# Cross-attention: keys scaled ahead of the last mask, the second chunk's transposes and evictions ahead of the values product, and a loop body of four batches

## The chip, the cores and the metric

The kernel runs on one core of a Trainium2 chip. A core has TensorE (PE, matrix products into the PSUM banks), VectorE (DVE), ScalarE (ACT), GpSimd (POOL) and SyncE (SP, which issues the transfers). Each engine works through a list of instructions of its own, in order, and semaphores tie the lists together. The metric is the device time of one launch in microseconds (us). The reader of a trace must know one habit of it: on PE an instruction's recorded duration overlaps the next one's start (a 512-column product is recorded as 0.39 us, and the next starts 0.23 us after it), so what PE loses is read from starts, or as recorded idle time plus that overlap of 0.17 us.

## What is computed

A decoder layer on 16 batches of 100 tokens, width 512: self-attention, cross-attention over 361 context tokens, and a routed feed-forward, each with a residual and a layer norm. The change touches cross-attention only:

```
q = rmsnorm((x @ Wq + bq) as 16 heads of 128) * qn_w
k = rmsnorm((ctx @ Wk + bk) as 4 heads of 128) * kn_w      # each shared by 4 query heads
v = (ctx @ Wv + bv) as 4 heads of 128
probs = softmax(q @ k^T / sqrt(128) + mask)
x = layernorm(x + (probs @ v) @ Wo)
```

## The kernel before

The program has three stages, one after another: self-attention, which also makes and stores the queries of cross-attention; cross-attention; feed-forward. In cross-attention the weights stay in SBUF and a loop runs over the 16 batches. Every product of precision is made in three passes, since each operand is kept as a high and a low part (`product3`, line 68): high x high, high x low, low x high. That is why each eviction comes twice: ACT writes the high part (`kTh`, `oTh`, `pTh`, `Vh`), then DVE subtracts it from the bank and writes the low part (`kTl`, `oTl`, `pTl`, `Vl`).

`body(j, par)` is written out by hand for each engine. It handles batch j in four steps s = 0 to 3, one for each of the four key heads and its four query heads. In a step, PE makes the scores of the four heads, and between them transposes the probabilities of the step before, in three chunks of 121 context tokens. DVE evicts each head's scores with the mask and takes the row's extreme (`masked`, line 1113), ACT takes the exponential and its sum (`exponent`, line 1010), DVE inverts the sums of two heads at a time (`invert_sums`, line 1119), and POOL scales the probabilities. After the fourth scores, PE makes the values product of the step before (`values_product`, three chunks by three passes, 9 matmuls), which ACT (line 1051) and DVE (line 1176) evict, and output products with `Wo` fill PE's time between.

The keys and values of the next batch are made inside the same steps, in three chunks c = 0, 1, 2 of 121 tokens. A key chunk goes this way:

- `keys(j + 1, c)` on PE, into one of two banks. Chunks 1 and 2 use the same bank, so chunk 2 waits until DVE has read chunk 1 (semaphore `k_ev`).
- `key_squares` on DVE: adds the bias (line 1076, which frees the bank), sums the squares (line 1081).
- `key_rsqrt` on POOL.
- `key_norm` on DVE (line 1089): scales the 121x512 chunk, 0.67 us.
- `transpose_keys` on PE (line 887): four transposes.
- `keys_hi` on ACT (line 995) and `keys_lo` on DVE (line 1095). The next batch's first scores wait for all three `keys_lo` (semaphore `kt_lo`).

In step 2 the chunk-0 keys are scaled, transposed, and then `keys(j + 1, 2)` is made. In step 3 chunks 1 and 2 are scaled and transposed. DVE also finishes the layer norm of the batch before: `apply_norm` (line 1240) in step 3, whose result SP stores (`x2_d`, line 818), and at the end of step 3 DVE waits until that store has landed (semaphore `x2_out`, line 1186), because it will write the same buffer again.

`over_batches` (line 727) sets which bodies are written out: batches 0 and 1, then a loop `Fori` of six rounds with two batches each (2 to 13), then 14, 15 and the rest of the last one. Every engine runs this loop with a branch of its own at line 732, taken five times and passed through the sixth time. Between the two branches of one round PE's list has 1,171 instructions (a matmul counted with its weight load), DVE's 312, ACT's 153, POOL's 123 and SP's 47. The loop of the self-attention stage (line 175) holds 218 on DVE.

## Time and profile before

| | us |
|---|---|
| median of 3 runs | 1598.19 |
| the runs | 1594.86 to 1598.56 |
| the profiled execution, its own time | 1600.98 |
| its span, first to last instruction | 1599.2 |
| self-attention, about | 0 to 530 |
| cross-attention, about | 530 to 1377 |
| feed-forward, about | 1377 to 1599 |

Over the span PE is busy 1475.6 us, its weight loads 1206.4, DVE 954.0, ACT 663.1 and POOL 649.0. The views used are the groups of waits of one engine, the timeline (instructions in order of time, with the idle time before one and what ended it in brackets), busy time by stretch, and the DMA queues of a stretch. Branches, register operations and waits that stand alone have no row in the timeline. They are seen only as idle time before the next row.

In the loop a batch takes 51 to 52 us, and batches 4, 6, 8, 10 and 12 are those that come right after a taken branch.

### The profile page before, as it was taken

How to read it: one execution, taken by the hardware profiler on the slowest of the kernel's cores; microseconds unless marked ns; L12 is line 12 of the kernel's file. 1: busy time of each engine (PE TensorE's matmuls, PEld its weight loads, DVE VectorE, ACT ScalarE, POOL GpSimd, SP SyncE). 2: the span in 40 equal slices, each digit the busy share in tenths (PEclk: the TensorE clock that was granted, in tenths of full speed). 3: DMA queues.
4: the chain of work that ended last, by engine and by line, in shares of the span. 5: the costliest groups of instructions: out<-in, count | busy, mean ns of one | idle time of the engine just before them, and what ended most of it. 6: DMA issues, size and time to landing. Idle time of an engine off the chain costs nothing. (4 is left out here: it accounts for less than half of the span.)

```text
span 1599.2 us, 27710 instructions
## 1 busy us (share of the span) xinstructions
PE 1475.6 (92%) x8462; PEld 1206.4 (75%) x8462; DVE 954.0 (60%) x3585; ACT 663.1 (41%) x1789; POOL 649.0 (41%) x1000
## 2 busy tenths in 40 slices
PE   6999999999988679999999999999999999479967
PEld 6777877877866468888888887888888888367844
DVE  3666566566566475566655665556555665753457
ACT  4443343333342253444444443444444445333346
POOL 1334334334334164344434444344434443364164
PEclk8999999999999899999999999999999999679988
DMA  6221221221232332111121212111121212465463
GB/s 207 105 73 62 92 72 61 92 72 61 88 111 73 123 111 71 57 59 55 42 60 55 64 39 64 60 55 54 42 60 55 64 48 105 174 195 152 143 215 103
DMA packets 60957, 139.75 MB, mean 87 GB/s; under 512 B 10182, under 2 KB 21034, under 8 KB 59876
## 3 DMA queue, kind: packets, MB, share of 16 engines
q1 hardware_dynamic: 56296, 123.85, 23.3%
q0 software_dynamic: 4576, 14.95, 3.5%
q8 instruction: 31, 0.51, 0.1%
q14 instruction: 54, 0.44, 0.1%
HBM read 94.31 MB, written 44.46 MB: 87 GB/s over the span
## 5 line engine op out<-in xcount | busy, mean ns | idle before, releaser
L1248 POOL TENSOR_TENSOR b_pcarry<-b_half 128x1 f32<-128x1 f32 x173 | 47.9, 277 | 394.5 <-DVE b_rinv L1119 356.9
L1010 ACT ACTIVATE b_probs<-b_probs,b_nmax 100x361 f32<-100x361 f32 x256 | 152.0, 594 | 81.3 <-DVE b_nmax L1113 80.9
L68 PE MATMUL bank<-b_kTh,b_q 128*100 128x362 f32 x512 | 171.6, 336 | 10.7 <-DVE b_kTl L1095 5.9
L1113 DVE CUSTOM_DVE_ANT_0 b_probs<-bank,b_mask 100x361 f32<-100x361 f32 x256 | 135.3, 529 | 53.8 <-issue 45.1
L1273 POOL TENSOR_SCALAR b_probs<-b_probs,b_rinv 100x361 f32<-100x361 f32 x256 | 163.1, 650 | 0.0
L1106 DVE TENSOR_TENSOR b_pTl<-bank,b_pTh 121x400 fp32r<-121x400 f32 x192 | 109.8, 572 | 49.1 <-ACT b_pTh L1005 49.0
L1005 ACT ACTIVATE b_pTh<-bank 121x400 fp32r<-121x400 f32 x192 | 96.8, 504 | 87.7 <-PE bank L849 82.9
L1051 ACT ACTIVATE b_oTh<-bank,b_bv 128x400 fp32r<-128x400 f32 x64 | 38.0, 594 | 228.8 <-PE bank L68 228.8
L849 PE MATMUL bank<-b_ident,b_probs 100*121 100x100 f32 x768 | 110.3, 266 | 6.6 <-POOL b_probs L1273 6.6
L849 PEld LDWEIGHTS bank<-b_ident,b_probs 100*121 100x121 f32 x768 | 108.0, 186 | 8.8 <-POOL b_probs L1273 7.9
L68 PE MATMUL bank<-b_Woh,b_oTh 128*100 128x512 f32 x256 | 111.4, 435 | 1.9 <-DVE b_oTl L1176 1.9
L68 PEld LDWEIGHTS bank<-b_kTh,b_q 128*100 128x100 f32 x512 | 84.8, 166 | 30.5 <-issue 13.6
L68 PE MATMUL bank<-a_Wqh,a_x1Th 128*100 128x512 f32 x256 | 100.8, 394 | 2.6 <-DVE a_qn L539 1.4
L68 PE MATMUL bank<-b_Woh,b_oTl 128*100 128x512 f32 x256 | 101.1, 395 | 0.0
L68 PE MATMUL bank<-b_Wol,b_oTh 128*100 128x512 f32 x256 | 101.0, 395 | 0.0
L68 PE MATMUL bank<-a_Wqh,a_x1Tl 128*100 128x512 f32 x256 | 101.0, 395 | 0.0
L68 PE MATMUL bank<-a_Wql,a_x1Th 128*100 128x512 f32 x256 | 100.6, 393 | 0.0
L1176 DVE SCALAR_TENSOR_TENSOR b_oTl<-bank,b_bv,b_oTh 128x400 fp32r<-128x400 f32 x64 | 40.5, 633 | 100.3 <-ACT b_oTh L1051 100.3
L416 ACT ACTIVATE a_probs<-a_probs,a_nmax 100x100 f32<-100x100 f32 x256 | 92.8, 366 | 4.4 <-DVE a_nmax L492 4.4
L619 POOL TENSOR_TENSOR a_probs<-a_probs,a_rinv 100x400 f32<-100x400 f32 x64 | 54.7, 855 | 93.0 <-DVE a_rinv L499 93.0
L68 PE MATMUL bank<-b_Wkh,b_ctxh 128*121 128x512 f32 x192 | 81.7, 426 | 11.3 <-DVE b_kn L1076 8.2
L68 PE MATMUL bank<-b_kTl,b_q 128*100 128x362 f32 x256 | 83.9, 328 | 0.0
(255 smaller groups left out, 3958.3 us busy)
## 6 DMA issues: line engine op xcount, KB each, us to landing
q_d<-a_qo SPq DMA_DIRECT2D x64, 400.0 KB, 2.4
b_q<-q_d SPq DMA_DIRECT2D x64, 400.0 KB, 3.1
b_ctxr<-in_ctxT SPq DMA_DIRECT2D x48, 242.0 KB, 3.8
y_d<-c_y SPq DMA_DIRECT2D x32, 256.0 KB, 3.6
c_Eraw<-in_expert_w SPq DMA_DIRECT2D x10, 512.0 KB, 12.2
a_stage<-in_Wq SPq DMA_DIRECT2D x4, 1024.0 KB, 6.0
stage<-in_Wo SPq DMA_DIRECT2D x8, 512.0 KB, 4.6
a_xTr<-in_xT SPq DMA_DIRECT2D x8, 400.0 KB, 3.2
```

Source lines behind the costliest of these rows:

```text
L68: mm = eng.matmul(out, lhsT=l(c), rhs=r(c), start=first and k == 0, stop=last and k == n - 1)
L416: e = act.activation(probs[:, r, c, :], probs[:, r, c, :], ACT.Exp, scale=-1.0, bias=nmax[:, h:h + 1], accum_out=psums[:, r, c:c + 1])
L619: pool.tensor_tensor(probs[:, r], probs[:, r], rinv[:, r].unsqueeze(2).to_broadcast([S, DC, S]), ALU.mult).then_inc(pn_rdy, 1)
L849: mm = pe.transpose(t_bank[c % 2][0:KT, h * S:(h + 1) * S], probs[:, s % 2, h, c * KT:(c + 1) * KT], ident_s[0:S, 0:S])
L1005: act.activation(pTh[:, c, :], t_bank[c % 2][0:KT, 0:XG * S], ACT.Copy).then_inc(pt_hi, 1)
L1010: act.activation(p, p, ACT.Exp, scale=-1.0, bias=nmax[:, s % 2, h:h + 1], accum_out=psums[:, s % 2, h:h + 1]).then_inc(e_rdy, 1)
L1051: act.activation(oTh[:, kv, :], o_bank[:, 0:XG * S], ACT.Identity, bias=bv_s[:, kv:kv + 1]).then_inc(o_hi, 1)
L1106: dve.tensor_tensor(pTl[:, c, :], t_bank[c % 2][0:KT, 0:XG * S], pTh[:, c, :].bitcast(F32), ALU.subtract).then_inc(pt_lo, 1)
L1113: dve.tensor_tensor_reduce(out=probs[:, s % 2, h, 0:SE], in0=s_bank[h % 2][0:S, 0:SE], in1=mask_s[:], scale=-1.0, scalar=BIG, op0=ALU.add, ...
L1176: dve.scalar_tensor_tensor(out=oTl[:, kv, :], in0=o_bank[:, 0:XG * S], scalar=bv_s[:, kv:kv + 1], in1=oTh[:, kv, :].bitcast(F32), op0=ALU.add,
L1248: pool.tensor_tensor(pcarry[:, k:k + 1], half_s[:, 0:1], half_s[:, 0:1], ALU.add)
L1273: pool.tensor_scalar(p, p, rinv[:, s % 2, h:h + 1], 1.0, ALU.mult, ALU.mult).then_inc(p_rdy, 1)
```

## The change

Three edits, all in cross-attention.

1. DVE, steps 2 and 3: `key_norm` of the next batch's chunk 0 (step 2) or chunk 1 (step 3) moves from behind the fourth `masked` and the first `invert_sums` to in front of that `masked`.
2. Step 3: the transposes of key chunk 1 move in front of the values product on PE, its `keys_hi` in front of the values product's eviction on ACT, its `keys_lo` in front of that on DVE. Chunk 2 stays where it was.
3. The loop takes four batches a round and three rounds, so its branch is taken twice. Its rounds then hold 2,337 instructions on PE, 618 on DVE, 299 on ACT, 241 on POOL and 91 on SP.

```diff
-            with eng.Fori(0, B // 2 - 2) as pair:
-                body(2 * pair + 2, 0)
-                body(2 * pair + 3, 1)
+            with eng.Fori(0, (B - 4) // 4) as quad:
+                for k in range(4):
+                    body(4 * quad + 2 + k, k % 2)
...
                     if s == 3:
                         output(j, 1, range(1, 2))
+                        if not last:
+                            transpose_keys(j + 1, 1)
                     if before:
                         values_product(n - 1, (s + 3) % 4, j)
...
                     if s == 3:
                         if not last:
-                            transpose_keys(j + 1, 1)
                             transpose_keys(j + 1, 2)
                         output(j, 1, range(2, XG))
...
+                    if s == 3 and not last:
+                        keys_hi(j + 1, 1, 1 - par)
                     if before:
                         kv = (s + 3) % 4
                         act.wait_ge(o_done, n)
...
                     if s in (2, 3) and not last:
-                        keys_hi(j + 1, s - 2, 1 - par)
-                    if s == 3 and not last:
-                        keys_hi(j + 1, 2, 1 - par)
+                        keys_hi(j + 1, 2 * (s - 2), 1 - par)
...
                     if now:
+                        if s in (2, 3) and not last:
+                            key_norm(j + 1, s - 2)
                         masked(j, s, 3)
                         invert_sums(j, s, 0)
-                        if s in (2, 3) and not last:
-                            key_norm(j + 1, s - 2)
                         invert_sums(j, s, 2)
...
                     if s == 3 and not last:
                         key_norm(j + 1, 2)
+                        keys_lo(j + 1, 1, 1 - par)
                     if before:
...
                     if s == 3 and not last:
-                        keys_lo(j + 1, 1, 1 - par)
                         keys_lo(j + 1, 2, 1 - par)
```

What this does to the lists is shown at three places. Line numbers of the changed kernel run one or two higher.

DVE in step 2, before, from the last `pTl` of the step to the bias add of key chunk 1 (the ISA rows of line 1113 are `masked`):

```order
L1106 TENSOR_TENSOR b_pTl<-bank,b_pTh 121x400 [waits b_pt_hi]
L1111 REGISTER_ALU
L1112 MEMSET b_carry 100x1 [waits b_s_done]
L1113 ISA b_probs,b_nmax<-bank,b_mask 100x361
L1113 ISA b_nmax 100x1
L1119 RECIPROCAL b_rinv<-b_psums 100x2 [waits b_e_rdy]
L1087 REGISTER_ALU
L1089 TENSOR_TENSOR b_kn<-b_kn,b_krs 121x512 [waits k_rs]
L1119 RECIPROCAL b_rinv<-b_psums 100x2 [waits b_e_rdy]
L1075 REGISTER_ALU
L1076 TENSOR_TENSOR b_kn<-bank,b_bk 121x512 [waits k_done]
```

and in the changed kernel:

```order
L1107 TENSOR_TENSOR b_pTl<-bank,b_pTh 121x400 [waits b_pt_hi]
L1088 REGISTER_ALU
L1090 TENSOR_TENSOR b_kn<-b_kn,b_krs 121x512 [waits k_rs]
L1112 REGISTER_ALU
L1113 MEMSET b_carry 100x1 [waits b_s_done]
L1114 ISA b_probs,b_nmax<-bank,b_mask 100x361
L1114 ISA b_nmax 100x1
L1120 RECIPROCAL b_rinv<-b_psums 100x2 [waits b_e_rdy] x2
L1076 REGISTER_ALU
L1077 TENSOR_TENSOR b_kn<-bank,b_bk 121x512 [waits k_done]
```

The scaling of the keys now stands ahead of the fourth `masked`, and the two reciprocals stand side by side.

DVE at the end of step 3, before, down to the loop's branch:

```order
L1240 TENSOR_SCALAR b_y<-b_y,b_mv,b_rstd 100x512 [waits b_rstd_set]
L1087 REGISTER_ALU
L1089 TENSOR_TENSOR b_kn<-b_kn,b_krs 121x512 [waits k_rs]
L1175 REGISTER_ALU
L1176 SCALAR_TENSOR_TENSOR b_oTl<-bank,b_bv,b_oTh 128x400 [waits b_o_hi]
L1095 TENSOR_TENSOR b_kTl<-bank,b_kTh 128x4x121 [waits kt_hi] x2
L732 REGISTER_ALU [waits x2_out]
L732 COMPARE_AND_BRANCH
```

and in the changed kernel:

```order
L1241 TENSOR_SCALAR b_y<-b_y,b_mv,b_rstd 100x512 [waits b_rstd_set]
L1088 REGISTER_ALU
L1090 TENSOR_TENSOR b_kn<-b_kn,b_krs 121x512 [waits k_rs]
L1096 TENSOR_TENSOR b_kTl<-bank,b_kTh 128x4x121 [waits kt_hi]
L1177 REGISTER_ALU
L1178 SCALAR_TENSOR_TENSOR b_oTl<-bank,b_bv,b_oTh 128x400 [waits b_o_hi]
L1096 TENSOR_TENSOR b_kTl<-bank,b_kTh 128x4x121 [waits kt_hi]
L732 REGISTER_ALU [waits x2_out]
L732 COMPARE_AND_BRANCH
```

One of the two `kTl` now stands ahead of `oTl`. The branch still stands behind a wait for the store.

PE in step 3, before, from the end of the values product on:

```order
L68 MATMUL bank<-b_pTh,b_Vl 128x400
L887 MATMUL bank<-b_ident,b_kn 128x121 [waits kt_lo,k_rdy]
L887 MATMUL bank<-b_ident,b_kn 128x121 x3
L887 MATMUL bank<-b_ident,b_kn 128x121 [waits k_rdy]
L887 MATMUL bank<-b_ident,b_kn 128x121 x3
L68 MATMUL bank<-b_Woh,b_oTh 100x512
```

and in the changed kernel, ahead of it:

```order
L68 MATMUL bank<-b_Woh,b_oTl 100x512
L887 MATMUL bank<-b_ident,b_kn 128x121 [waits kt_lo,k_rdy]
L887 MATMUL bank<-b_ident,b_kn 128x121 x3
L856 REGISTER_ALU
L68 MATMUL bank<-b_pTh,b_Vh 128x400 [waits b_o_lo,b_pt_lo]
L68 MATMUL bank<-b_pTl,b_Vh 128x400
```

Four of the eight transposes now come before the nine matmuls of the values product, the other four stay behind them. PE's six output matmuls still end the step.

## Rows read from the trace of the kernel before

**Rows 1.** The page: engines' busy time over the span, share and instructions.

```profile
PE 1475.6 (92%) x8462; PEld 1206.4 (75%) x8462; DVE 954.0 (60%) x3585; ACT 663.1 (41%) x1789; POOL 649.0 (41%) x1000
```

**Rows 2.** Busy by stretch: PE, PEld, DVE, ACT, POOL; then PE's clock, DMA.

```profile
850.00:950.00 100.00, 98.23 (x541) 82.77 (x540) 59.55 (x222) 41.61 (x107) 43.64 (x82) 1.00 0.19 56
```

**Rows 3.** PE's waits, 560 to 1370 us: total, times, longest.

```profile
PE bank L68 <- DVE b_kn L1076: 8.2, 15, 3.5
...
PE bank L68 <- DVE b_kTl L1095: 4.2, 12, 0.4
PE bank L68 <- DVE b_nmax L1113: 3.8, 5, 1.1
...
PE bank L887 <- DVE b_kn L1089: 1.9, 1, 1.9
```

**Rows 4.** Timeline, PE, batch 5, step 2: start, duration, instruction, idle before.

```profile
841.04 0.39 PE L68 MATMUL bank<-b_Woh,b_oTl 128*100 128x512 f32 x1
841.36 0.63 PE L887 MATMUL bank<-b_ident,b_kn 121*128 121x121 f32 x4
842.33 0.47 PE L68 MATMUL bank<-b_Wkh,b_ctxh 128*121 128x512 f32 x1 [0.34 <-DVE b_kn L1076]
```

**Rows 5.** Timeline, DVE and one row of ACT, the same step.

```profile
839.42 0.57 DVE L1106 TENSOR_TENSOR b_pTl<-bank,b_pTh 121x400 fp32r<-121x400 f32 x1 [0.40 <-ACT b_pTh L1005]
840.10 0.53 DVE L1113 CUSTOM_DVE_ANT_0 b_probs<-bank,b_mask 100x361 f32<-100x361 f32 x1
...
840.63 0.68 DVE L1089 TENSOR_TENSOR b_kn<-b_kn,b_krs 121x512 f32<-121x512 f32 x1
841.39 0.17 DVE L1119 RECIPROCAL b_rinv<-b_psums 100x2 f32<-100x2 f32 x1
841.49 0.69 DVE L1076 TENSOR_TENSOR b_kn<-bank,b_bk 121x512 f32<-121x512 f32 x1
...
841.17 0.18 ACT L1010 ACTIVATION_READ_ACCUMULATOR b_probs<-b_probs,b_nmax 100x1 f32 x1
```

**Rows 6.** Timeline, batch 5, end of step 3: DVE, ACT, PE.

```profile
854.31 0.67 DVE L1089 TENSOR_TENSOR b_kn<-b_kn,b_krs 121x512 f32<-121x512 f32 x1
855.93 0.64 DVE L1176 SCALAR_TENSOR_TENSOR b_oTl<-bank,b_bv,b_oTh 128x400 fp32r<-128x400 f32 x1 [0.94 <-ACT b_oTh L1051]
856.48 1.22 DVE L1095 TENSOR_TENSOR b_kTl<-bank,b_kTh 128x484 fp32r<-128x484 f32 x2
...
855.30 0.59 ACT L1051 ACTIVATE b_oTh<-bank,b_bv 128x400 fp32r<-128x400 f32 x1 [1.73 <-PE bank L68]
855.79 1.03 ACT L995 ACTIVATE b_kTh<-bank 128x484 fp32r<-128x484 f32 x2
...
855.10 0.99 PE L887 MATMUL bank<-b_ident,b_kn 121*128 121x121 f32 x8
...
857.08 0.40 PE L68 MATMUL bank<-b_Woh,b_oTl 128*100 128x512 f32 x1
857.83 0.40 PE L68 MATMUL bank<-b_kTh,b_q 128*100 128x362 f32 x1 [0.36 <-DVE b_kTl L1095]
```

**Rows 7.** Timeline around a taken branch: the store's issue, DVE's return, PE's wait.

```profile
854.42 0.34 SPq L818 DMA_DIRECT2D x_d<-b_y  x1
...
861.35 0.06 DVE L1112 MEMSET b_carry<- 100x1 f32 x1 [3.66 <-PE bank L68]
...
862.00 0.41 PE L68 MATMUL bank<-b_kTh,b_q 128*100 128x362 f32 x1 [0.38 <-DVE b_nmax L1113]
```

**Rows 8.** DMA queues: instruction packets from 603 to 755, then from 755 to 1262.

```profile
q8 instruction: 7, 0.11, 0.3%
...
q14 instruction: 24, 0.20, 0.1%
```

**Rows 9.** Busy by stretch as in rows 2: a gap of PE, and after it.

```profile
579.50:583.50 4.00, 0.61 (x5) 0.38 (x4) 3.13 (x4) 1.87 (x2) 4.00 (x5) 0.96 0.43 120
583.50:587.00 3.50, 3.43 (x9) 2.68 (x10) 1.02 (x8) 0.00 (x0) 1.52 (x3) 0.55 0.69 263
```

## The prediction

> **What bounds the kernel now.** First the page: PE has by far the most busy time [rows 1]. Then busy time by stretch inside the cross-attention loop: PE 98 of 100 us at its full clock, 2.4 GHz (1.00 in the column), DVE 60, ACT 42 [rows 2]. So PE is the bound of this stage. The change takes no work from it, and can only move the time in which PE stands still. PE's waits list that time by cause [rows 3]. Three causes recur. (a) Step 2 of every batch: the product of key chunk 2 waits until DVE has read chunk 1 out of the bank, 15 times for 8.2 us, of which one, in batch 0, is 3.5, so 0.34 recorded on the others. (b) The first scores of a batch wait for `kTl`: 0.36 recorded at the row, about 14 times (12 of them are listed). (c) The scores of head 2 wait for `nmax`: 3.8 us in 5 times. With the overlap of 0.17 us that a recorded idle time leaves out, (a) costs 0.51 us, (b) 0.52 and (c) 0.93 each time. Cause (c) has as many cases as the loop has taken branches, and the row shows it right behind one.
>
> **Edit 1, step 2: `key_norm` ahead of the fourth `masked`.** Follow (a) back. The product starts at 842.33 [rows 4], 0.15 behind the end of DVE's bias add (841.49 + 0.69 = 842.18), which follows the second reciprocal at 841.39 [rows 5]. Two things end there in the kernel before: `key_norm` (840.63 + 0.68 = 841.31) and ACT's exponential of head 3 (841.17 + 0.18 = 841.35). The later is the exponential, and its chain starts with the fourth `masked` at 840.10. In the new order `key_norm` starts where `pTl` leaves DVE, at 839.42 + 0.57 - 0.08 = 839.91 (neighbours on DVE overlap by some 0.08), holds it for 0.60, and `masked` starts at about 840.52, 0.42 later than before. Exponential, reciprocal, bias add and the product behind them all move by that 0.42. Nothing absorbs it, since PE is already waiting. The transposes of chunk 0 get their keys sooner (840.6 for 841.3), but they lie in front of the same wait and win only 0.09 of it, which becomes wait. Batches 1 to 14: 14 x 0.42 = **+5.9**. Batch 0 waits at the same place and once more before the chunk-2 transposes (the 3.5 and the 1.9 [rows 3]). Both hang on DVE work behind that exponential: **+0.8**. Bounds for the 14: nothing if the order on DVE did not matter, and 14 x 0.68 = 9.5 if it moved by the whole scaling. The start at 839.91 is read, so I take 5.9.
>
> **Edits 1 and 2, step 3.** Here `masked` is late by the same 0.42, and with it the reciprocals, `apply_norm` and `key_norm` of chunk 2 (854.31 becomes 854.74, end 855.41). PE does four transposes in 4 x 0.103 = 0.41 (the eight take 0.99 with the last one's drain [rows 6]) ahead of the values product. So that product ends 0.41 later, ACT's `oTh` starts at 855.71 for 855.30, and DVE's `oTl` at 856.34 for 855.93. In return one `kTl` (0.56 of DVE) has gone from behind `oTl` to in front of it, where DVE stood idle for 0.94. Last `kTl` before: 856.48 + 1.22 = 857.70. After: 856.34 + 0.55 + 0.66 = 857.55. ACT's last `kTh` (start 856.20, end 856.78) is in time for that. The wait shrinks by 0.15 of its 0.52, not by all of it: what moved off DVE's tail (0.56) came back as a late product (0.41). PE's work ends at 857.08 + 0.23 = 857.31 either way. Chunk 2's transposes need their keys at 855.5 and have them at 855.45. That is a tie, and a tenth late would be hidden in the wait. Twelve batch ends, without the two at which the branch is still taken: 12 x -0.15 = **-1.8**. POOL scales its last two heads at most 0.4 later than before, and its cover is more than 1 us.
>
> **Edit 3, the branches that go.** Behind a branch DVE's next row comes after 3.66 us of idle time, at 861.35 [rows 7], though the scores it wants were ready at about 858.6 (three passes from 857.83 [rows 6]). PE runs on until head 2 and loses 0.93 on average. Three of five branches go (into batches 4, 8 and 12): 3 x -0.93 = **-2.8**. What DVE does in the gap is seen in the DMA queues. From 755 to 1262 us the queue of 8 KB instruction packets moves 24 [rows 8], about five to a round, so a list of the loop is brought in again each round. It is DVE's, the one that returns late, with 312 instructions. From 145 to 440 us, inside the self-attention loop with DVE's 218, that queue has no row.
>
> **Edit 3, the two branches that stay.** DVE reaches its branch only when the store is in. It is issued at 854.42 [rows 7], and I put its landing near 857, where the last `kTl` starts [rows 6]. `apply_norm` is 0.42 later, so the return is too, and without more these two branches cost 2 x 0.43 = **+0.9**. But PE's own list is now 2,337 instructions a round. The queue of 16 KB packets, which serves PE, moved 7 from 603 to 755 us, up to the first branch, and has no row at all from 755 to 1262 [rows 8], so 1,171 instructions stay on the chip. Whether 2,337 do, no row shows. Bounds: nothing (they stay), or a return like DVE's. PE's sequencer is some 2.2 us ahead of its array (an estimate from the 26 instructions that lie queued there), so it takes the branch at about 855.1. DVE's return takes 4.3 us (857.05, the start of the last `kTl`, to 861.35), and I add 0.9 for a packet of twice the size and the loads that are under way then. PE would start at 860.3 to 860.4, so it stands still for 3.1 us from 857.31 instead of 0.52. That is longer than DVE's gap, which is then hidden, as is any return of ACT. And a gap of that size drops the clock: after PE's idle time in batch 0, most of the 4.0 us from 579.5, the granted clock averaged 0.55 over 3.5 us [rows 9], which puts it at 1.2 GHz for most of them and costs 0.45 x 3.5 = 1.6. Sum per branch: 3.1 + 1.6 - (0.52 + 0.93) = 3.25, for two **+6.5**. I take this end: a list that has doubled is nearer to DVE's, which no longer fitted with 312 where 218 did, than to one that stays.
>
> The Trainium skill, page "Runtime: NRT & Kernel Launch", section "Instruction fetch mechanics", bears on this in two ways. It says that kernels prefer full unrolling, because a taken branch whose target has left the buffer forces a fetch: that speaks for the edit, and for the three branches removed the trace agrees (0.93 each). It also gives PE's buffer as 2048 instructions and the others' as 512. By the first figure 2,337 would not fit and the +6.5 would stand. By the second DVE's 312 would have fitted, and the trace denies that with the 3.66 us.
>
> **The sum.** 5.9 + 0.8 - 1.8 - 2.8 + 6.5 = +8.6. On the profiled execution (1600.98, span 1599.2) that gives 1609.6. That execution lies 2.8 above the median of the runs, and the forecast is made on the median: 1598.2 + 8.6 = **1606.8**.
>
> **The rivals.**
> - **PE's round stays on the chip.** 5.9 + 0.8 - 1.8 - 2.8 + 0.9 = +3.0, so 1601.2, not slower by what can be told. For it: PE keeps nearly four times DVE's round today, and no row shows its limit. Against it: the list doubles, and DVE's limit lay within a factor of 1.4 (218 to 312).
> - **PE fetches, but the clock holds.** +8.6 - 3.2 = +5.4: 1603.6. The clock stood at 1.00 through the stretch that holds PE's wait at 862.00 [rows 2, 7], and the computed 3.1 could come out smaller, since DVE's return is its only row.
> - **The move of `key_norm` is free, and the tail wait goes altogether** (the faster side). If `masked` had slack after all, (a) stays as it is, and if the values product were not late, (b) falls to zero: -14 x 0.52 - 2.8 + 0.9 = -9.2, so 1589. It decides at the point where `masked` can start before 840.1, and the row has DVE freed only at 839.9. Half of it (only the first) gives -1.8 - 2.8 + 0.9 = -3.7: 1594.5.
> - **The fetches collide.** PE, ACT and DVE all return within 3 us and into the loads of queries and context. The returns of today differ (the longest wait of (c) is 1.1 where the mean is 0.76 [rows 3]), and three at a time could take 2 us more each: 1598.2 + 8.6 + 2 x 2 = 1611.
>
> **How the numbers follow.** Forecast 0.48, branch stays on the chip 0.22, clock holds 0.13, collision 0.07, the free move 0.10 (0.05 for each half). About 0.3%, 4.8 us, is what a measurement of this kernel can tell from no change, which puts the line at 1603.0. Faster: 0.05. Same: the rival of 1601.2, the half at 1594.5, half of the 1603.6 and a little of the forecast's spread, 0.35. Slower: 0.60. The range reaches from just under the first rival to the collision: 1599.5 to 1611. It leaves out the free move and part of the collision.
>
> **What the changed profile would show.** Edit 1 is right if (a) reads about 0.76 recorded instead of 0.34, with `masked` right behind `kn` on DVE. Step 3 is right if (b) reads about 0.2 recorded and `oTh` starts 0.6 behind the transposes of chunk 1. The branch is right if (c) is gone at batches 4, 8 and 12, and at batches 6 and 10 PE stands still for about 3 us at its first scores, with 16 KB instruction packets inside the loop and a clock below 1.00 behind the gap. Without 16 KB packets in the loop the first rival holds. The forecast is wrong as a whole if (a) keeps its 0.34.

## The result and the profile after

| | before | changed |
|---|---|---|
| median, us | 1598.1 (7 runs) | 1605.31 (7 runs) |
| lowest to highest | 1593.33 to 1599.51 | 1601.88 to 1608.0 |
| span of the profiled execution | 1599.2 | 1605.0 |

The changed kernel takes 1.0051 of the time of before, with a 95% interval of 1.0037 to 1.0066. It is 7.2 us slower by the medians, where +8.6 and a time of 1606.8 were forecast.

The page first. The busy times have hardly moved from [rows 1]; PE's grew by 4.0 us, which later turns out to be mostly clock, and the span grew by 5.8.

```profile
PE 1479.6 (92%) x8462; PEld 1210.5 (75%) x8462; DVE 960.1 (60%) x3585; ACT 666.7 (42%) x1789; POOL 637.5 (40%) x1000
```

So the loss is idle time of PE, and the next view is PE's waits from 560 to 1380 us (what it waits for, total, times, longest), to be laid beside [rows 3].

```profile
PE bank L68 <- DVE b_kn L1077: 16.8, 15, 4.3
PE bank L68 <- issue: 4.9, 3, 2.4
PE bank L887 <- DVE b_kn L1090: 2.9, 1, 2.9
...
PE bank L68 <- DVE b_kTl L1096: 0.2, 1, 0.2
```

Cause (a), the product that waits for the bias add, has doubled: 16.8 us for 8.2. Of that, one case, in batch 0, is 4.3, and the other 14 have 0.89 each instead of 0.34. Cause (b), `kTl`, is nearly gone from the list. Cause (c), `nmax`, is gone from it. In its place stands "issue": time in which PE waited for nothing that the profile shows, 2.4 us at the longest.

**Step 2 of batch 5**, on PE, DVE and ACT, beside [rows 4, 5]; the columns are start, duration, instruction, and idle time before it:

```profile
842.73 0.40 PE L68 MATMUL bank<-b_Woh,b_oTl 128*100 128x512 f32 x1
842.97 0.58 PE L887 MATMUL bank<-b_ident,b_kn 121*128 121x121 f32 x4
844.44 0.47 PE L68 MATMUL bank<-b_Wkh,b_ctxh 128*121 128x512 f32 x1 [0.89 <-DVE b_kn L1077]
...
841.11 0.57 DVE L1107 TENSOR_TENSOR b_pTl<-bank,b_pTh 121x400 fp32r<-121x400 f32 x1 [0.40 <-ACT b_pTh L1006]
841.60 0.68 DVE L1090 TENSOR_TENSOR b_kn<-b_kn,b_krs 121x512 f32<-121x512 f32 x1
842.21 0.53 DVE L1114 CUSTOM_DVE_ANT_0 b_probs<-bank,b_mask 100x361 f32<-100x361 f32 x1
...
843.50 0.17 DVE L1120 RECIPROCAL b_rinv<-b_psums 100x2 f32<-100x2 f32 x1 [0.68 <-ACT b_probs L1011]
843.60 0.69 DVE L1077 TENSOR_TENSOR b_kn<-bank,b_bk 121x512 f32<-121x512 f32 x1
...
842.78 0.60 ACT L1011 ACTIVATE b_probs<-b_probs,b_nmax 100x361 f32<-100x361 f32 x1 [1.13 <-DVE b_nmax L1114]
```

`masked` starts 1.10 behind `pTl` (842.21 - 841.11); before it was 0.68 (840.10 - 839.42). The shift is 0.42, as worked out. The scaling no longer stands in DVE's wait for the exponential: the second reciprocal now comes after 0.68 us of idle time. DVE did its 0.68 us of scaling ahead of that chain and then stood idle for as long, with PE waiting behind it.

**The taken branch into batch 6**, PE and DVE, the end of step 3 and the return:

```profile
857.45 0.34 PE L68 MATMUL bank<-b_pTh,b_Vl 121*128 121x400 f32 x1
857.78 0.63 PE L887 MATMUL bank<-b_ident,b_kn 121*128 121x121 f32 x4
...
859.41 0.40 PE L68 MATMUL bank<-b_Woh,b_oTl 128*100 128x512 f32 x1
862.23 0.40 PE L68 MATMUL bank<-b_kTh,b_q 128*100 128x362 f32 x1 [2.42 <-issue]
...
856.26 0.86 DVE L1241 TENSOR_SCALAR b_y<-b_y,b_mv,b_rstd 100x512 f32<-100x512 f32 x1
857.05 0.67 DVE L1090 TENSOR_TENSOR b_kn<-b_kn,b_krs 121x512 f32<-121x512 f32 x1
857.64 0.65 DVE L1096 TENSOR_TENSOR b_kTl<-bank,b_kTh 128x484 fp32r<-128x484 f32 x1
858.46 0.64 DVE L1178 SCALAR_TENSOR_TENSOR b_oTl<-bank,b_bv,b_oTh 128x400 fp32r<-128x400 f32 x1 [0.17 <-ACT b_oTh L1054]
859.05 0.66 DVE L1096 TENSOR_TENSOR b_kTl<-bank,b_kTh 128x484 fp32r<-128x484 f32 x1
864.17 0.06 DVE L1113 MEMSET b_carry<- 100x1 f32 x1 [4.45 <-issue]
```

DVE has its last `kTl` done at 859.71, and PE's work ends at 859.64 (859.41 + 0.23). Nothing that PE needs is missing after 859.71, and yet its first scores come at 862.23. DVE comes back later still, at 864.17, but in the shadow of PE's gap it costs nothing more: no `nmax` wait is left. The queues of instruction packets, from 755 to 1270 us (packets, MB, share), tell what PE was doing:

```profile
q8 instruction: 26, 0.43, 0.3%
q14 instruction: 28, 0.23, 0.2%
```

The queue that serves PE had no row inside the loop before [rows 8]. Now it has 26 packets of 16 KB there: PE's list of 2,337 instructions is brought in again. (Packets alone don't tell of a stall, as a version without a loop shows below. It is the two together, the packets and PE's gap at the branch.)

The second taken branch, into batch 10, is the same on PE. The window behind it shows the clock (busy time of PE, PEld, DVE, ACT, POOL; then PE's clock, DMA):

```profile
1066.26 0.40 PE L68 MATMUL bank<-b_Woh,b_oTl 128*100 128x512 f32 x1
1068.97 0.40 PE L68 MATMUL bank<-b_kTh,b_q 128*100 128x362 f32 x1 [2.31 <-issue]
1070.64 0.63 PE L68 MATMUL bank<-b_Wol,b_oTh 128*100 128x512 f32 x1
...
1069.00:1073.00 4.00, 4.00 (x17) 3.48 (x18) 1.09 (x4) 1.31 (x3) 0.00 (x0) 0.58 0.17 57
```

Behind a gap of 2.3 us the granted clock averaged 0.58 over 4 us, 1.2 GHz for most of them; behind the gap of 2.4 us in front of batch 6 it stayed at 1.00.

**The time by batch**, from the first scores of one batch to the next one's, read off the timeline of both traces:

| batch | before | changed | difference |
|---|---|---|---|
| 0 | 48.89 | 51.85 | +2.96 |
| one without a branch | 50.82 | 51.12 | +0.30 |
| right behind a branch that went (4, 8, 12) | 52.13, 52.04, 51.60 | 51.12, 51.09, 51.08 | -1.01, -0.95, -0.52 |
| 5 and 6 (branch that stays) | 50.83, 51.42 | 53.54, 51.09 | +2.38 |
| 9 and 10 (branch that stays) | 50.81, 51.82 | 53.43, 52.67 | +3.47 |

Cross-attention as a whole went from 817.9 to 826.3 us, +8.4 (554.70 to 1372.62, and 553.60 to 1379.90). The span grew by less, 5.8, since the two other stages, whose code is the same, came out shorter in this execution by 1.1 and 1.5.

### The profile page after: what moved, and what is told of

It is laid out like the page before. It is cut to its first block and busy times, and to the rows that moved or that the text cites. A ratio compares the mean times of both kernels' runs of the same rounds, so it can differ in the third digit from the quotient of the medians.

```text
span 1605.0 us, 27650 instructions
## 1 busy us (share of the span) xinstructions
PE 1479.6 (92%) x8462; PEld 1210.5 (75%) x8462; DVE 960.1 (60%) x3585; ACT 666.7 (42%) x1789; POOL 637.5 (40%) x1000
## 5 line engine op out<-in xcount | busy, mean ns | idle before, releaser
L1249 POOL TENSOR_TENSOR b_pcarry<-b_half 128x1 f32<-128x1 f32 x173 | 43.1, 249 | 405.7 <-DVE b_rinv L1120 367.9
L1274 POOL TENSOR_SCALAR b_probs<-b_probs,b_rinv 100x361 f32<-100x361 f32 x256 | 155.5, 621 | 0.0
L68 PE MATMUL bank<-b_Wkh,b_ctxh 128*121 128x512 f32 x192 | 81.7, 426 | 18.3 <-DVE b_kn L1077 16.8
```

The costliest lines, as they stand in the source:

```text
L68: mm = eng.matmul(out, lhsT=l(c), rhs=r(c), start=first and k == 0, stop=last and k == n - 1)
L1249: pool.tensor_tensor(pcarry[:, k:k + 1], half_s[:, 0:1], half_s[:, 0:1], ALU.add)
L1274: pool.tensor_scalar(p, p, rinv[:, s % 2, h:h + 1], 1.0, ALU.mult, ALU.mult).then_inc(p_rdy, 1)
```

## Experiments

Each was timed in five rounds beside the kernel before. "Ratio" is the time over that of before, with its 95% interval.

### The two halves of the change alone

**The loop alone**: the kernel before with the loop of four batches.

```diff
-            with eng.Fori(0, B // 2 - 2) as pair:
-                body(2 * pair + 2, 0)
-                body(2 * pair + 3, 1)
+            with eng.Fori(0, (B - 4) // 4) as quad:
+                for k in range(4):
+                    body(4 * quad + 2 + k, k % 2)
```

> The kernel before with the four-batch loop alone. My theory: PE's round of 2,337 instructions has to be brought in again at each of the two taken branches, whatever DVE does. Then batches 4, 8 and 12 lose the 3.3 us that they stood behind a branch, the batch ends ahead of 6 and 10 show PE idle for about 3 us with 16 KB instruction packets in the loop, and these two cost 4 to 5 us more than before: +1.4 us in all (0 to +3). Rival: the gap of the changed kernel came from DVE, whose return was late because apply_norm and the store were. Then it is gone here and the loop alone gives -3 us, with PE's first scores of batches 6 and 10 on time.

Measured: 1597.28 us, ratio 1.0002 (0.9985 to 1.0020). PE's list is brought in here too, with the order of instructions otherwise as before (first PE at the branch, then the queue from 755 to 1262):

```profile
856.75 0.40 PE L68 MATMUL bank<-b_Woh,b_oTl 128*100 128x512 f32 x1
858.67 0.40 PE L68 MATMUL bank<-b_kTh,b_q 128*100 128x362 f32 x1 [1.53 <-issue]
...
q8 instruction: 26, 0.43, 0.4%
```

The mechanism holds; the size doesn't. The batches that end at a branch take 51.99 and 52.35, so the two gaps cost 1.2 and 1.5 more than a batch without one. That is 1.1 more than these two branches cost before, where 4 to 5 had been expected. The clock stays at 1.00 behind both, and the three branches that went pay for them: over batches 2 to 13 the trace is 2.2 us shorter, which the times, with an interval of 3 us either way, neither show nor exclude. The raw records of the trace, which the views leave out, show where the smaller gap comes from: PE reaches its branch 2.1 us ahead of the end of its work here, and 1.7 in the changed kernel. The branch itself takes 3.4 and 3.8 us here and 3.9 and 3.8 there, so the lead explains 0.4 of each gap's difference (1.7 and 2.0 beyond the end of work here, 2.6 and 2.5 there), and at the first of them the longer return adds another 0.5.

What sets the lead can be read too. In all eight traces with a loop PE's branch comes 0.20 to 0.25 us behind the end of DVE's scaling of chunk 2, which PE's transposes wait for (in the changed kernel 857.05 + 0.67 = 857.72, and the branch at 857.93). The lead is 2.1 in the kernel before and in this one, 1.7 in all four with the scaling of chunk 1 moved in front of `masked` in step 3, which makes chunk 2's later, and 2.3 where only the transposes are moved.

**The scaling alone**: the kernel before with `key_norm` in front of the fourth `masked`.

```diff
                     if now:
+                        if s in (2, 3) and not last:
+                            key_norm(j + 1, s - 2)
                         masked(j, s, 3)
                         invert_sums(j, s, 0)
-                        if s in (2, 3) and not last:
-                            key_norm(j + 1, s - 2)
                         invert_sums(j, s, 2)
```

> The kernel before with the move of key_norm alone (two-batch loop, chunk 1 as before). My theory: the product of key chunk 2 waits 0.42 to 0.46 us longer in each of 14 batches (6.2), batch 0 adds 0.8 or more, and each of the five taken branches returns 0.42 later, since the store that DVE waits for is later (2.1): +9 us (+7 to +11). Rival: the longer wait of the changed kernel came from the chunk-1 transposes ahead of the values product. Then this run is within 2 us of the kernel before and the wait for b_kn stays at 0.34 recorded.

Measured: 1607.42 us, ratio 1.0065 (1.0050 to 1.0081). PE's waits:

```profile
PE bank L68 <- DVE b_kn L1076: 16.8, 15, 4.3
PE bank L68 <- DVE b_nmax L1113: 5.8, 5, 1.5
PE bank L68 <- DVE b_kTl L1095: 1.4, 7, 0.3
```

The first row is that of the changed kernel to the tenth. The second shows the price of the late `apply_norm`, which I had put at 0.43 a branch: the wait behind branches grew from 3.8 us to 5.8 in five, 0.4 each. In the raw records DVE takes its branch 0.16 us ahead of the next batch's first scores, where it was 0.80 before. So this one edit carries the loss of the changed kernel.

**Step 2 put back**: the changed kernel, but in step 2 the scaling stands behind `masked` again.

```diff
                     if now:
-                        if s in (2, 3) and not last:
-                            key_norm(j + 1, s - 2)
+                        if s == 3 and not last:
+                            key_norm(j + 1, 1)
                         masked(j, s, 3)
                         invert_sums(j, s, 0)
+                        if s == 2 and not last:
+                            key_norm(j + 1, 0)
                         invert_sums(j, s, 2)
```

> The changed kernel with key_norm of chunk 0 back behind the fourth masked, step 3 and the four-batch loop as changed. My theory: the longer wait for b_kn is all step 2's, so a batch takes 50.6 us for 51.1 (0.51 of stand for 1.06, with the shorter batch end kept), and the two taken branches still cost 4 to 6 us. Against the changed kernel -7 to -9 us, so 1597 or a little less, the time of the kernel before. Rival: what step 3's order does (masked and the transposes moved there) costs as much as step 2's. Then a batch stays above 50.9 us and the kernel above 1600.

Measured: 1599.09 us, ratio 1.0007 (0.9994 to 1.0019), with PE's waits:

```profile
PE bank L68 <- DVE b_kn L1077: 8.2, 15, 3.5
PE bank L68 <- issue: 4.5, 3, 2.3
```

Cause (a) is back at its 8.2. Putting one call back behind `masked` gives back 6.2 us of the 7.2 by the medians, a little less than the 7 to 9 expected. A batch without a branch takes 50.65 to 50.72, less than the 50.82 before: what was changed in step 3 is, taken together, a small gain when nothing is late in step 2. In batch 0 (a) is back to 3.5, yet the batch stays long (51.97): the wait at `L887`, which belongs to step 3, keeps the 2.9 of the changed kernel.

**The second chunk alone**: step 3's transposes and evictions in front, pair loop, scaling behind `masked` as before. Its diff is the middle part of the change's own.

```diff
                     if s == 3:
                         output(j, 1, range(1, 2))
+                        if not last:
+                            transpose_keys(j + 1, 1)
...
+                    if s == 3 and not last:
+                        keys_hi(j + 1, 1, 1 - par)
...
                     if s == 3 and not last:
                         key_norm(j + 1, 2)
+                        keys_lo(j + 1, 1, 1 - par)
```

> The kernel before with chunk 1's transposes and evictions ahead of the values product alone. My theory: the wait for kTl at the batch end falls by 0.15 to 0.3 us, but the transposes now want key_norm of chunk 1 at the moment when it ends (853.5 in the trace of before), which gives some 0.1 back: -1 to -3 us in all. Rival: without key_norm moved as well the transposes stand waiting in front of the values product, and the kernel is slower by 1 us or more.

Measured: 1597.25 us, ratio 1.0002 (0.9987 to 1.0016): no difference that can be told. In the trace the first scores of a batch wait less than the 0.36 of [rows 6], but a batch without a branch still takes 50.81 for 50.82:

```profile
802.38 0.41 PE L68 MATMUL bank<-b_kTh,b_q 128*100 128x362 f32 x1 [0.20 <-DVE b_kTl L1096]
...
PE bank L68 <- DVE b_nmax L1114: 2.1, 5, 0.5
```

The 0.16 that the tail gained was lost ahead of it: with the values product first, PE had no wait for chunk 1's keys; with chunk 1's transposes first, it has one of about 0.1, as expected. What remains of the gain stands at the branches, where 3.8 us of `nmax` waits became 2.1. Why is open: DVE takes its branch where it did, 0.79 us ahead of the next batch's first scores for 0.80, and only what comes behind it is shorter (4.1 to 4.3 us to its next raw record, for 4.2 to 4.9).

### What a taken branch costs

**No loop before**: the kernel before with all twelve batches written out, so without a branch in cross-attention.

```diff
-            with eng.Fori(0, B // 2 - 2) as pair:
-                body(2 * pair + 2, 0)
-                body(2 * pair + 3, 1)
+            for j in range(2, B - 2):
+                body(j, j % 2)
```

> The kernel before with the 12 batches of the loop written out one after another, no branch. My theory: all five returns go and nothing takes their place, since straight code is brought in ahead of its use: batches 4, 6, 8, 10 and 12 take 50.8 us like the others, -4.9 us (-4 to -6). Rival: code that is never used twice has to be brought in all the time and starves an engine, which would show as gaps at several places of a batch and a time like that of before or longer.

Measured: 1590.33 us, ratio 0.9950 (0.9935 to 0.9965). No batch shows a gap at its start, all take 50.70, and the `nmax` wait is gone. Of the 6.3 us that the trace gains over batches 2 to 13, 4.9 is what the five branches cost before and 1.4 is twelve times 0.12, which each batch takes less. The instruction packets from 755 to 1262 show that new instructions come in all the time, and no batch takes longer for them:

```profile
q8 instruction: 23, 0.38, 0.3%
q14 instruction: 18, 0.15, 0.1%
```

Hence the packets as such are no sign of a stall. In these traces PE stood still for its instructions only behind a taken branch whose round had not stayed on the chip.

**No loop after**: the changed kernel with the batches written out (the same edit, on the loop of four).

```diff
-            with eng.Fori(0, (B - 4) // 4) as quad:
-                for k in range(4):
-                    body(4 * quad + 2 + k, k % 2)
+            for j in range(2, B - 2):
+                body(j, j % 2)
```

> The changed kernel with the 12 batches written out, nothing else. It tells what the loop still costs it. My theory: the two taken branches stand for 5 to 6 us of PE's time, and register work for 0.1 us a batch, so -6 to -8 us against the changed kernel: 1598, about the time of the kernel before, and a batch still takes 51.0 us because of the moved key_norm. Rival: the branch costs of the changed kernel were mostly the clock of one execution, and the two branches are worth 3 us or less: 1602.

Measured: 1597.9 us, ratio 1.0006 (0.9992 to 1.0019), and (a) is as in the changed kernel:

```profile
PE bank L68 <- DVE b_kn L1076: 16.3, 15, 4.3
```

The loop's two branches and its counters cost the changed kernel 7.4 us by the medians (1605.31 - 1597.9); in the trace batches 2 to 13 gained 7.9, of which each of the twelve has 0.15 (50.97 for 51.12).

**The wait ahead of the branch**: the kernel before, with DVE's wait for the store of `x2` moved from the end of step 3 to just ahead of `residual_norm` in the next step that writes the buffer, behind the branch.

```diff
-                    if s == 3 and not first:
-                        dve.wait_ge(x2_out, 16 * j)
...
+                if not (isinstance(j, int) and j == 0):
+                    dve.wait_ge(x2_out, 16 * j)
                 dve.wait_ge(x1_in, 16 * (j + 1))
                 dve.wait_ge(y_done, j + 1)
```

> The kernel before with one wait of DVE moved: the wait for the store of x2, which stood at the end of step 3 in front of the branch, now stands in front of the next write of that buffer (step 1 of the next batch). My theory: DVE's branch is held by that store, so it now comes about 0.5 us sooner, DVE returns sooner, and PE's wait for nmax behind the five taken branches falls from 0.93 us to about 0.45: -2.4 us (-1 to -4), seen in the trace. Rival: DVE's return is set by the transfer of its instructions, which waits for the loads of queries and context under way then. An earlier branch gains nothing and the five waits stay.

Measured: 1598.48 us, ratio 0.9998 (0.9986 to 1.0011), so the 2.4 us expected can't be seen in the time. The `nmax` waits and DVE's return:

```profile
PE bank L68 <- DVE b_nmax L1113: 2.5, 5, 0.8
...
862.81 0.06 DVE L1112 MEMSET b_carry<- 100x1 f32 x1 [3.73 <-PE bank L68]
```

The waits fell from 3.8 us to 2.5, but the store is not shown to be the reason. In the raw records DVE's branch lies 0.89 us ahead of the next batch's first scores where it was 0.80, so the store had held it by 0.09 and not by half a microsecond. The rest is the way from the branch to DVE's next record, 4.4 us on average for 4.5, and that way differs by 0.7 among the five branches of the kernel before (4.16 to 4.85). The run with the second chunk alone has the store's wait in place and waits of 2.1.

### Improving on both

**The bias add in front**: cause (a) is the product waiting for the bias add, which stands behind the second reciprocal. The bias add itself needs neither the exponential nor the reciprocal. Here the changed kernel does it ahead of that reciprocal, in DVE's wait for ACT.

```diff
+            def key_bias(jn, c):
+                dve.wait_ge(k_done, 3 * jn + c + 1)
+                dve.tensor_tensor(kn[:, c % 2, :], key_bank(jn, c)[0:KT, :], bk_s[:], ALU.add).then_inc(k_ev, 1)
...
                         masked(j, s, 3)
                         invert_sums(j, s, 0)
+                        if s == 2 and not last:
+                            key_bias(j + 1, 1)
                         invert_sums(j, s, 2)
...
-                        key_squares(j + 1, s - 1)
+                        key_squares(j + 1, s - 1, s == 1)
```

The last argument of `key_squares` says whether the bias add is still to be done there.

> The changed kernel (four-batch loop) with one instruction of DVE more moved in step 2: the bias add of key chunk 1, which frees the bank, in front of the second reciprocal, so behind masked and not behind the exponential of head 3. My theory: the wait for b_kn is the chain masked, exponential, reciprocal, bias add. Without the middle of it PE stands 0.2 us for 1.06, a batch takes 50.3 us, and the kernel -11 us against the changed one: 1594 (1591 to 1597). Rival: the wait only moves on, to the squares or to the probabilities of heads 2 and 3, which POOL scales later. Then another wait of PE appears in step 3 and the time stays above 1600.

Measured: 1590.37 us, ratio 0.9960 (0.9944 to 0.9975), a little below the range expected. No wait of cause (a) is left in PE's list. A batch without a branch takes 50.2 to 50.3, 0.9 less than in the changed kernel. Batch 0 takes 45.04, almost 7 us less than there: in it the bias add had stood behind DVE's splits of `Wo` as well. That it would, I had not counted. The branches still cost 2.0 and 3.8 (52.19, then 52.53 and 51.78). The profiled execution, 1583.14 us, is the fastest of the eight, so its trace flatters the kernel: the median lies 7.2 above it.

**Bias add in front, no loop**: the same with the batches written out.

```diff
-            with eng.Fori(0, (B - 4) // 4) as quad:
-                for k in range(4):
-                    body(4 * quad + 2 + k, k % 2)
+            for j in range(2, B - 2):
+                body(j, j % 2)
```

> The kernel of the run before, with the 12 batches written out one after another. My theory: what the two taken branches cost (6.3 us in the trace of the changed kernel) and some 0.1 us a batch for register work go, so 1586 (1583 to 1590), the fastest of all. Rival: with PE's waits so short another engine is late where it was not, and it is no better than the straight kernel with the old order (1590).

Measured: 1578.54 us (1577.44 to 1584.24), ratio 0.9891 (0.9872 to 0.9910). It beats both kernels, and it misses its forecast of 1586 (1583 to 1590) on the fast side. That forecast started from the 1594 expected of the run above, which came to 1590.37; from there writing the loop out gives 11.8 by the medians, though the traces show only 6.9 over batches 2 to 13. Where the other 5 come from isn't shown. The window of [rows 2], then DVE and PE in step 2, then PE from one batch to the next:

```profile
850.00:950.00 100.00, 99.65 (x553) 84.70 (x552) 61.47 (x228) 43.53 (x111) 43.23 (x82) 1.00 0.19 57
...
830.39 0.67 DVE L1074 TENSOR_TENSOR b_kn<-bank,b_bk 121x512 f32<-121x512 f32 x1
831.15 0.17 DVE L1124 RECIPROCAL b_rinv<-b_psums 100x2 f32<-100x2 f32 x1
...
830.61 0.58 PE L886 MATMUL bank<-b_ident,b_kn 121*128 121x121 f32 x4
831.20 0.47 PE L68 MATMUL bank<-b_Wkh,b_ctxh 128*121 128x512 f32 x1
...
846.52 0.38 PE L68 MATMUL bank<-b_kTh,b_q 128*100 128x362 f32 x1 [0.16 <-issue]
```

The product for chunk 2 now starts with no idle time noted in front of it, and the bias add stands ahead of the reciprocal, which used to hold it. PE is busy for 99.65 of 100 us. A batch without a branch takes 50.13.

**Step 3 as before, in that version**: the same again, but chunk 1's transposes and evictions, and its scaling, in their old places.

```diff
                         masked(j, s, 3)
                         invert_sums(j, s, 0)
+                        if s == 3 and not last:
+                            key_norm(j + 1, 1)
                         invert_sums(j, s, 2)
...
                     if s == 3:
                         output(j, 1, range(1, 2))
-                        if not last:
-                            transpose_keys(j + 1, 1)
```

> The straight kernel with the bias add first and with step 3 as in the kernel before (key_norm of chunk 1 behind the fourth masked, its transposes and evictions behind the values product). It tells what the step-3 part of the change is worth. My theory: the batch end goes from 0.33 us of stand back to about 0.5, so +0.15 to +0.2 us a batch and +2 to +3 us against the straight kernel with the bias add first (1578.5): 1581. Rival: step 3's two moves cancel (masked later, tail shorter), and the batch takes 50.13 us as there.

Measured: 1580.54 us, ratio 0.9900 (0.9880 to 0.9920). In its trace the wait at the batch's start is back:

```profile
845.83 0.40 PE L68 MATMUL bank<-b_Woh,b_oTl 128*100 128x512 f32 x1
846.54 0.38 PE L68 MATMUL bank<-b_kTh,b_q 128*100 128x362 f32 x1 [0.32 <-issue]
```

A batch takes 50.27 for 50.13. The step-3 part of the change is worth 0.14 a batch in this trace. By the medians it is 2.0 us, which is below what the timing of two such kernels can separate (their intervals overlap). In batch 0 it works the other way: with the old step 3 it takes 43.75 for 44.89, and the wait at its chunk-2 transposes is 2.1 for 3.2.

## Why the prediction was right, point by point

The time fell into the range, and the sum of the terms in the traces is near the forecast, +8.4 for +8.6. Two of the terms were off by about 2 us each, in opposite directions, so that closeness is in part luck. In the table "measured" is from the batch times and rows of the two traces; the first two rows are read within a batch without a branch.

| term | forecast | measured |
|---|---|---|
| step 2, 14 batches | +5.9 | +5.7 (14 x 0.41) |
| batch ends (forecast for 12, measured for 14) | -1.8 | -1.4 (14 x -0.10) |
| step 2 and batch ends together, by batch times | +4.1 | +4.2 (14 x 0.30) |
| batch 0 | +0.8 | +3.0 |
| three branches that went | -2.8 | -3.4 |
| two branches that stay | +6.5 | +4.65 |
| sum, first scores of batch 0 to those of batch 15 | +8.6 | +8.4 |

- **Step 2.** Right. `masked` starts 0.42 later behind `pTl`, and nothing absorbs it. From a batch's first scores to the product of chunk 2 PE takes 35.74 us in batch 5 (808.70 to 844.44) where it took 35.32 (807.01 to 842.33), 0.42 more, and 0.41 in the batches without a branch. The two starts, before and changed:

```profile
807.01 0.40 PE L68 MATMUL bank<-b_kTh,b_q 128*100 128x362 f32 x1 [0.36 <-DVE b_kTl L1095]
```

```profile
808.70 0.40 PE L68 MATMUL bank<-b_kTh,b_q 128*100 128x362 f32 x1
```

  (a) went from 0.34 recorded to 0.89, where 0.76 was said. Of the 0.55, 0.42 is the shift and 0.09 is from the transposes that come sooner, which I had named but not added to what the row would read; the rest is in the record, where the transposes' row ends 0.05 sooner (0.58 for 0.63). The scaling alone and the step put back both show it: 16.8 and 8.2 us of wait, and the time follows (1.0065, and 1.0007 with the step put back).
- **Batch ends.** Right in direction, with a tie that fell the wrong way. The tail wait shrank from 0.52 to 0.22, twice the 0.15 forecast. But the tie, keys at 855.45 for transposes at 855.5, was lost: `apply_norm` took 0.86 us where I had read 0.69. Chunk 2's transposes start 0.33 behind the last values product where they started 0.18 behind it, and by the output product behind them PE has lost 0.20. "A tenth late would be hidden in the wait" was wrong: the tail's gain of 0.30 less these 0.20 is the 0.10 that the rest of a batch gains (15.40 us from the product of chunk 2 to the next batch for 15.50). The chunk alone loses its 0.16 in the same way. `oTh` starts at 857.83, behind the last part of the values product, much as said.
- **The branches that went.** Right: the `nmax` wait is gone at batches 4, 8 and 12. They cost 1.3, 1.2 and 0.8 in batch time before (52.13, 52.04 and 51.60 against 50.82), where I had taken the average wait, 0.93, for each. Written out, the kernel before gains 4.9 at five.
- **The branches that stay.** The mechanism is right and its size was too big by 1.8. PE's list is brought in again at each of the two, PE stands still with all its operands there, and DVE's return is hidden behind it. Three numbers in it were mis-sized. First, the return: I gave PE DVE's 4.3 us and 0.9 more for the larger packets, 5.2, and from its branch to its first product it takes 4.3 and 4.2. At batch 6 the raw records have it whole: the branch at 857.93, taken until 861.84, some register instructions, and the first product at 862.23. So the 0.9 was not there. Second, the lead: PE takes the branch 1.71 us ahead of its work's end at 859.64, where I had said 2.2. The 2.2 is that of the kernel before. I had worked out myself that chunk 2 is scaled 0.43 later, and did not carry that to the branch, which follows this scaling by 0.2. Together the gap is 4.30 - 1.71 = 2.6 us beyond the end of work, and 2.5 at the other branch, for 3.1. Third, the clock: it fell behind one of them and not behind the other, so 1.6 us that I had counted twice came once (the second branch's batch has +1.55). These would make 2.7 less than forecast, 1.1 for the gaps and 1.6 for the clock. Some 0.9 of it comes back, since the old cost was 0.80 on average and not 0.93, and since a changed batch without a branch, the measure here, has a tail 0.3 shorter. By the batch times the two branches cost 2.42 and 3.86 where they cost 0.60 and 1.00. The Trainium skill gives, on its page "Runtime: NRT & Kernel Launch", section "Instruction fetch mechanics", 2048 instructions as PE's buffer: the trace agrees, 1,171 stayed on the chip and 2,337 did not. For the other engines it gives 512; here DVE with 312 and ACT with 299 come back late, and POOL with 241 does not, so a round of fewer than 512 is not sure to stay.
- **Batch 0.** The step that failed: I took 0.4 for each of its two waits, the shift of `masked` alone, and nothing for its clock. (a) went from 3.5 to 4.3 and the wait at `L887` from 1.9 to 2.9, which makes 1.8. The shift of 0.4 is in each of them, but the DVE work behind that exponential got longer as well: the split of `Wo` (`b_Wol`, `L1068` before and `L1069` changed) takes 2.6 us for 2.4 each time, and chunk 2's scaling 0.97 for 0.68 in the second. Why they do isn't shown. Most of the rest is the clock, as two windows of the whole batch show, before and changed:

```profile
554.70:603.60 48.90, 37.82 (x184) 31.39 (x185) 33.69 (x109) 25.29 (x55) 28.90 (x39) 0.90 0.36 112
```

```profile
553.60:605.45 51.85, 39.87 (x184) 33.17 (x185) 34.36 (x109) 25.28 (x55) 27.69 (x39) 0.84 0.34 108
```

  PE has the same 184 instructions, takes 2.05 us longer for them, and the mean clock of 0.90 became 0.84. Against these 3.9 us stands a wait of 0.95 for POOL's probabilities that the changed kernel no longer has. The batch times of the other runs tell whose doing the +3.0 is. In the four traces with the scaling of chunk 1 ahead of `masked` in step 3 and the old bias add, batch 0 takes 50.99 (scaling alone), 51.85 (changed), 51.97 (step 2 put back) and 52.63 (changed, no loop), and the wait at `L887` is 2.9 in all. In the five without it takes 47.63 to 49.36, and that wait is 1.7 to 1.9. So most of the +3.0 goes with the moved scaling, and with its step-3 half at least, since the batch is as long with step 2 put back. How much of it is the clock of a single execution stays open: there is one trace of each kernel.
- **The rivals.** That PE's round stays on the chip (1601.2) fell with the 26 packets. That the clock holds (1603.6) came true at one branch of two, and at all four with the loop alone and with step 2 put back; the measured 1605.31 lies between it and the forecast. The free move fell with the 0.42. The collision didn't come: PE's return takes 4.3 and 4.2 us where I had reckoned 5.2 without any collision.

What stays open: why the clock fell behind the second gap of 2.3 us and not behind the first of 2.4, why the way from a branch to the next instruction differs from branch to branch (on DVE by 0.7 us in the kernel before), and how much of batch 0's loss is its clock.

## What to carry to other kernels

Ask of each instruction moved forward on an in-order engine which chain stands behind it: the scaling was moved out of a wait of DVE, where it cost nothing, to the front of the chain of mask, exponential, reciprocal and bias add that PE was waiting for, and PE paid its shift in full in each of 14 batches. Better was to find the work at the end of that chain that didn't need it (the bias add) and to do that in the wait. A longer loop body takes fewer branches but may push another engine's list out of the chip, so look at the instruction queues and at the largest list first; here writing the loop out entirely was worth 0.5%, where the loop of four batches alone gained nothing (1.0002).

## What the runs showed of the hardware

- A list that does not fit is brought in again at every taken branch, and each engine has its own limit: PE kept 1,171 instructions and not 2,337. Of the smaller engines POOL kept 241 (its next raw record is 0.3 us behind the branch) and ACT 153 (0.24 to 0.26), while ACT's 299 and DVE's 312 came back late. PE's branch takes 3.4 to 3.9 us in the four traces with the loop of four and 0.2 in those with the loop of two. DVE's idle time is 3.66 to 4.45 us in the kernel before and the changed one. ACT's next raw record in the changed kernel is 3.7 us behind its branch (858.52 to 862.20), close behind PE's return and hidden by it.
- Straight code is brought in while it runs, one 16 KB packet each 22 us (23 in 507 us), with 50.67 to 50.71 us in each of the twelve batches.
- The time by which PE's branch lies ahead of the end of its work comes off what bringing the list in costs. It cost 1.2 to 1.5 us of batch time where the branch lay 2.1 us ahead, and 2.0 to 2.4 where it lay 1.7 ahead (changed kernel, step 2 put back, bias add in front), before any clock. The branch came 0.20 to 0.25 us behind the end of DVE's scaling of chunk 2 in all eight traces with a loop.
- Gaps of much the same length were followed by different clocks. A recorded gap of 2.31 us was followed by 0.58 over 4 us, and one of 2.42 by 1.00, in the same execution. With step 2 put back, one of 2.27 was followed by 1.00; with the bias add in front, one of 2.31 by 0.57.
